# GAT passes of a GNN kernel: the softmax chain spread over six steps, everything behind it two steps later

## The reference

```python
h = relu(layernorm(x))
for m in range(3):
    g = h @ W[m]; s = g @ a_src[m]; d = g @ a_dst[m]
    e = leaky_relu(s[src] + d[dst], 0.2)            # edges and a self-loop for every node
    w = exp(e - segment_max(e, dst)[dst])
    alpha = w / (segment_sum(w, dst)[dst] + 1e-16)
    h = h + sigmoid(segment_sum(alpha[:, None] * g[src], dst) + b[m])
x = x + h
```

## Time and profile before

| what | value |
|---|---|
| median of 3 timed runs | 6098.72 us (6097.92 to 6103.44) |
| profiled execution, span | 6863.7 us |
| TensorE busy | 5226.3 us (76%) |
| VectorE busy | 4349.7 us (63%) |
| ScalarE busy | 3453.8 us (50%) |
| GpSimd busy | 3591.8 us (52%) |
| GAT passes 0, 1, 2 (us from the span's start) | 2223 to 2836, 2843 to 3568, 3568 to 4347 |

### The profile page before, as it was taken

How to read it: one execution, slowest core, us unless ns; L and a number is a source line. 1 busy time by engine, 2 the same in 40 slices (tenths; PEclk the granted TensorE clock), 3 DMA queues, 4 the chain that set the end, 5 groups by cost and what they waited for, 6 DMA issues and landing times. The chain is left out here.

```text
span 6863.7 us, 100426 instructions
## 1 busy us (share of the span) xinstructions
PE 5226.3 (76%) x23898; PEld 3081.0 (45%) x23898; DVE 4349.7 (63%) x11924; ACT 3453.8 (50%) x7591; POOL 3591.8 (52%) x3533
## 2 busy tenths in 40 slices
PE   4899999999947567546763788699989976666665
PEld 2566666666522333223331444466656643333332
DVE  7788888888747777657773888455545534434343
ACT  4788888888748445425551556332323323222222
POOL 3444444444224563266626553466566645677776
PEclk9999999999979678767785889899989988889888
DMA  9988877776557555435543677566567753333332
GB/s 212 272 281 277 282 261 241 239 240 230 195 176 231 147 164 166 131 111 165 164 152 113 223 238 253 160 184 184 181 192 228 231 180 102 106 108 110 107 108 77
DMA packets 909509, 1274.04 MB, mean 186 GB/s; under 512 B 248502, under 2 KB 398967, under 8 KB 902579
## 3 DMA queue, kind: packets, MB, share of 16 engines
q1 hardware_dynamic: 696170, 1063.92, 47.3%
q0 software_dynamic: 112896, 202.19, 12.2%
q10 hardware_dynamic: 100016, 3.20, 1.2%
HBM read 623.49 MB, written 654.07 MB: 186 GB/s over the span
## 5 line engine op out<-in xcount | busy, mean ns | idle before, releaser
L1734 POOL DMA_INDIRECT n_xs<-table,look x1176 | 1175.0, 999 | 742.0 <-issue 316.1
L1876 DVE TENSOR_TENSOR_SCAN n_dT<-n_km,n_dT,bank 128x512 f32<-128x512 uint8 x291 | 372.4, 1280 | 1293.9 <-DMA dots<-g_dt 655.8
L1439 POOL DMA_INDIRECT g_xs<-table,look x784 | 775.9, 990 | 752.7 <-POOLq L206 260.9
L626 POOL DMA_INDIRECT p_rows<-in_x_dram,dst_ix x392 | 386.0, 985 | 564.4 <-DMA raw_rows<-p_rows 285.8
L634 POOL DMA_INDIRECT table<-slot_pair,map_ix x392 | 397.1, 1013 | 463.9 <-ACT n_sg L742 253.5
L1836 ACT ACTIVATE n_eT<-bank,edge_b 128x512 f32<-128x512 f32 x294 | 202.0, 687 | 831.0 <-PE bank L1778 467.9
L670 PE MATMUL bank<-n_xT,gat_w 128*128 128x512 f32 (+1 forms) x1176 | 559.8, 613 | 53.9 <-issue 38.6
L1746 POOL DMA_INDIRECT out_dram<-n_xn,n_row_of x392 | 463.0, 1181 | 262.3 <-issue 123.6
L689 PE MATMUL bank<-n_zT,wn 128*128 128x512 f32 (+1 forms) x1176 | 539.2, 594 | 15.4 <-issue 8.6
L1829 ACT ACTIVATE n_sT<-bank 128x512 f32<-128x512 f32 x294 | 175.5, 597 | 659.0 <-DMA g_sc<-far_rows 431.1
L1557 ACT ACTIVATE g_xw<-g_xs,g_cols 128x128 f32<-128x128 f32 x1176 | 370.7, 387 | 126.4 <-PE bank L1507 80.8
(11 more groups left out here) (274 smaller groups left out, 12424.0 us busy)
## 6 DMA issues: line engine op xcount, KB each, us to landing
table<-n_ro SPq DMA_DIRECT2D x768, 256.0 KB
g_gb<-decays SPq DMA_DIRECT2D x294, 256.0 KB
n_xd<-table SPq DMA_DIRECT2D x294, 256.0 KB
table<-g_xn SPq DMA_DIRECT2D x196, 256.0 KB
g_xo<-table SPq DMA_DIRECT2D x196, 256.0 KB
edge_feats<-n_eT SPq DMA_DIRECT2D x196, 256.0 KB
table<-n_xn SPq DMA_DIRECT2D x196, 256.0 KB
n_ea<-edge_feats SPq DMA_DIRECT2D x196, 256.0 KB
```

What stands on the lines that cost most here:

```text
L626: q.indirect_dma_start(out=edge_rows[e % UX][:, u, :], out_offset=None, in_=x, in_offset=bass.IndirectOffsetOnAxis(ap=dst_ix[:, t:t + 1], ...
L1439: q.indirect_dma_start(out=xs[g % XR][:, u, :], out_offset=None, in_=tables[l], in_offset=bass.IndirectOffsetOnAxis(ap=src_ix[:, t:t + 1] ...
L1734: q.indirect_dma_start(out=xs.buffers[g % UE][:, u, :], out_offset=None, in_=tables[L], in_offset=bass.IndirectOffsetOnAxis(ap=look[:, t, ...
L1876: V.tensor_tensor_scan(in_order(dT[g][:, :]), kept(g), in_order(flat_banks[1]), 0.0 if begins(g) else carry(dT[g.before(1)]), ALU.mult, AL ...
```

## The change

All pieces of the softmax chain move to other lags, mostly one piece a step; everything behind the chain moves two steps later; on each engine the order inside a step changes; ring `xs` of passes 1 and 2 has 22 buffers in place of 20; and the gathers' wait for `columns` of superstep 0 moves from group SG + 3 to SG + 6. The functions themselves are unchanged.

```diff
@@ -1053,7 +1053,7 @@
-            XR, OR = FIRST if l == 0 else 20, 9
+            XR, OR = FIRST if l == 0 else 22, 9
@@ -1343,9 +1343,9 @@
-                        flat(GE, [(6, logits), (7, arguments), (8, sum_carry), (9, columns), (5, source_dots), (17, add_self),
-                                  (6, max_carry), (7, sums), (8, shares), (19, sum_edges)]
-                             + ([(24, stats), (24, scales)] if last_layer else [(22, new_rows)]))
+                        flat(GE, [(6, logits), (7, max_carry), (8, arguments), (5, source_dots), (19, add_self), (21, sum_edges)]
+                             + ([(26, stats), (26, scales)] if last_layer else [(24, new_rows)])
+                             + [(8, sums), (9, sum_carry), (10, shares), (11, columns)])
@@ -1414,10 +1414,10 @@
-                        flat(GE, [(0, load_own_scalars), (6, store_own_scalars), (8, load_scalars),
-                                  (9, store_decays), (17, load_decays), (15, load_own)]
-                             + ([(17, load_raw), (20, load_marks), (24, store_rows), (32, store_normed)] if last_layer
-                                else [(23, store_rows), (25, store_dots)]))
+                        flat(GE, [(0, load_own_scalars), (6, store_own_scalars), (9, load_scalars),
+                                  (11, store_decays), (19, load_decays), (17, load_own)]
+                             + ([(19, load_raw), (22, load_marks), (26, store_rows), (34, store_normed)] if last_layer
+                                else [(25, store_rows), (27, store_dots)]))
@@ -1432,7 +1432,7 @@
-                            elif g == SG + 3:
+                            elif g == SG + 6:
@@ -1543,9 +1543,10 @@
-                        flat(GE, [(6, max_to_row), (8, sums_to_column), (18, turn), (20, multiply)]
-                             + [(5, dots_to_rows), (6, max_to_column), (7, sums_to_row), (8, to_columns)]
-                             + ([(22, join_rows)] if last_layer else [(23, turn_back), (24, dot)]))
+                        flat(GE, [(20, turn), (22, multiply), (9, sums_to_row), (10, sums_to_column), (11, to_columns)]
+                             + ([(24, join_rows)] if last_layer else [(25, turn_back)])
+                             + [(5, dots_to_rows), (6, max_to_row), (7, max_to_column)]
+                             + ([] if last_layer else [(26, dot)]))
@@ -1603,8 +1604,8 @@
-                        flat(GE, [(7, weights), (16, scale)] + ([(23, join)] if last_layer else [(20, add_half)]) + [(21, gate)]
-                             + ([(31, normalise)] if last_layer else [(23, copy_back), (24, copy_dots)]))
+                        flat(GE, [(18, scale), (8, weights)] + ([(25, join)] if last_layer else [(22, add_half)]) + [(23, gate)]
+                             + ([(33, normalise)] if last_layer else [(25, copy_back), (26, copy_dots)]))
```

## The result

The changed kernel takes 6133.09 us in the median of 4 runs, against 6099.6 us of the kernel before; the medians are 33.5 us apart. Forecast was 6097 with a range up to 6122.

The account below looks back on a forecast made before the run. Gathers were taken to bound pass 1, VectorE passes 0 and 2. Added steps +16, pause -6 and chain -11 us sum to -1, so 6097 us, range 6045 to 6122.

Parts of the forecast that it names:

- What bounds each pass: GAT passes, freed of waits: pass 1 bound by gathers (5.10 us over 4.7), passes 0 and 2 by VectorE.
- The long waits: VectorE's waits at softmax-chain lines: mostly absent from timed runs; if all were real, -135 us (rival, chance 0.27).
- the rule on the gap: Skill's rule: a profile exceeds executed time by about 6.2 us whatever the kernel, so the waits would be in timed runs.
- Added steps: Two more steps between gather and result: 0 in pass 0, +5.7 in pass 1, +10.2 in pass 2; sum +16.
- The pause: GpSimd's idle before gather 13 in passes 1 and 2: 4.5 us falls to some 2; 3 each taken, -6.
- The spread: Softmax chain, about one step between product and reader: 0.4 us saved per superstep in VectorE-bound passes, -11.
- TensorE's order: TensorE's step in pass 2: dots_to_rows now stands behind join_rows' six products, 2.6 us later; priced only in rival (b).
- rival (b): Pass 2: TensorE's new order delays the chain, VectorE waits at L1168; +36, half +18; total 6127; chance 0.12.

Follow-up runs that it names:

- before_again: The kernel before, unchanged, profiled a second time: 6103.87 us, span 6102.1 us.
- steps_only: Kernel before with everything behind the chain two steps later and a ring of 22; chain, its order and the pause as before: ratio 1.003.
- products_early: Changed kernel with dots_to_rows, max_to_row and max_to_column ahead of join_rows and turn_back in TensorE's step: ratio 1.0007 against the kernel before.
- before_late: Kernel before with max_to_column alone moved behind join_rows and turn_back in TensorE's step: ratio 1.0038.
- column_early: Changed kernel with max_to_column alone moved ahead of join_rows and turn_back in TensorE's step: ratio 0.9998 against the kernel before.

## Why the prediction was wrong, point by point

**What bounds each pass: right.** Pass 1 is paced by the gathers: in the second profile of before, VectorE waits for gathers in the middle of the pass, and 392 gathers of 1.01 us and 0.305 us between them make 516 of its 596 us. Passes 0 and 2 are paced by VectorE: its last dots come 57 and 37 us behind the start of the last gather, against 6 us in pass 1. Only the gathers' rate was taken too fast: 1.275 us each in the first profile's window, 1.316 in this one's pass 1.

**The long waits are foreign to the timed runs: right**, by before_again. Of the two reasons given, that the gather-free stretches had none stands. The other, that the operand was there by the record, is weaker than it was put: the end of the product at 3205.47 is modelled, and the trace has its semaphore update at 3215.45, right before VectorE's restart at 3215.47. By that update it was TensorE's result that came late, for a cause that stays open. By the rule on the gap the waits would have been in the timed runs; they were not. The Trainium skill ("Runtime: NRT & Kernel Launch", section "The ~15µs preamble/postamble breakdown") has a profile's total about 6 us above the executed time. No run here agrees: in before_again and the changed kernel the span is 1.8 and 1.7 us below the time, and in the first profile it is 765 us above it, which marks that profile as unfit for costing waits.

**Added steps: right in sign, 2 to 4 us short in each pass.** Forecast 0, +5.7 and +10.2; steps_only has +4, +8 and +14. In pass 2 the first `join` (L1570) starts 12.1 us later than before (118.8 against 106.7 us into the pass), near the +10.2. The 2 full steps that were to pay for the 2 drain steps paid 14.3 us (from there to the last dots 418.6 against 432.9), while the part behind the last dots grew by 16.1 (109.6 against 93.5), in part because a superstep's norm scales moved into the drain as well (four sets of them stand there, three before). What pass 0 loses was not looked into.

**The pause: right.** Forecast 4.5 us falling to 2; measured, GpSimd's waits in pass 1, before (second profile) and changed:

```profile
POOL g_xs L1439 <- DVE g_cols L1257: 6.1, 1, 6.1
```

```profile
POOL g_xs L1439 <- DVE g_cols L1257: 2.9, 1, 2.9
```

3.2 us here and 2.6 in pass 2 (5.5 to 2.9), forecast 3 each. The idle before gather 13 was to be 2 to 6 us; it is 2.9.

**The spread: right in size, by pass.** Forecast -11 for passes 0 and 2 together, and the pause -3 in pass 2; products_early less steps_only gives -9 and -6, so about -12 without the pause. By all terms together pass 0 was forecast at -6 (measured -5), pass 1 at +3 (+2), pass 2 at +2 (+31).

**TensorE's order: this step failed.** The forecast's sum has no term for it. It was left to rival (b) with a chance of 0.12, whose price (+36, half of it +18) and ground (TensorE's 4.42 us against VectorE's 3.84 in pass 2) were right: the reordering costs 23 us of pass 2 (664 against 641). Two things were wrong in it. The place: logits and L1462 were named, and the waits there stayed at 1.0 us; it was L1476, the last product of TensorE's step, read by the first VectorE piece of the next. The check to make was, for each of the six products, what stands between it and its reader on both engines; L1476 had VectorE's lightest chain step (0.2 us of `max_carry`) to cover TensorE's longest. And the argument against, that the norm scales in the step before let TensorE catch up: it did catch up, idled for about 3 us, and started the step that mattered at the lower clock.

How much of the wait is the clock? before_late has the same products in the same order at the upper clock, 4.57 us and a wait of 0.9. An estimate from it: with 4.57 us in place of 7.25 the changed kernel's step would have ended at 3522.2, as VectorE arrived, so in this kernel nearly all of the 2.8 us is the lower clock. The place is what lets it reach VectorE: with L1476 ahead of the block the same idles cost next to nothing (column_early). No run held the clock fixed in the changed kernel itself.

The range ended at 6122, below the 6127 of (b), as (b) had a chance of only 0.12. The steps of 4.42 and 3.84 us stood in rows at hand; no row there showed the slower step behind an idle.

## What to carry to other kernels

When a chain hops between two in-order engines, list for every hop what stands between producer and reader on both queues; spreading the pieces over steps helps nothing if one product moves behind the longest block of its engine. A tiny product is late by everything ahead of it, so put it first in the step and the block last. Slack in front of a block is no safe cover either: TensorE's idle of 3 us was followed by a step of 7.25 us in place of 4.57. And where a profile is over a tenth longer than the timed runs, take another before costing a wait from it.

## What the runs showed of the hardware that was not expected

One profiled execution of the same kernel took 6863.7 us and the next 6102.1. In the long one VectorE and ScalarE often resumed together, as at 3215.47 and 3215.53 after 8.48 and 9.65 us of idle, and every wait of VectorE over 3.5 us in the GAT passes fell where GpSimd was issuing gathers. Why is open.

A TensorE idle of 3.00 us was followed by products at half rate for about 5 us (L1517 2.08 us for 1.16, L1527 1.92 us for 1.02, granted clock 0.50), and TensorE was late for the next hop. Idles of one length weren't always followed alike: behind 2.54 us in before_late all six join products were slow in four supersteps, a part of them in six, and none in one.

The same 392 gathers of pass 2 kept GpSimd busy for 378.26 us before and 397.72 us in the changed kernel, 0.965 and 1.015 us each, though the instructions are the same. It seems to cost little here, as VectorE paces this pass: column_early has 396.75 us of gathers and a pass of 638. Why they lengthen was not tried.
